# Cross-attention with 16 heads: masks written into the score banks by ScalarE, and held with all 64 keys on 64 rows

## What is computed

```python
# x (4, 1024, 256), ctx (4, 64, 256), mask (4, 1024, 64) of 0 and 1; 16 heads of 16
Q = split_heads(x @ w_q.T + b_q);  K = split_heads(ctx @ w_k.T + b_k);  V = split_heads(ctx @ w_v.T + b_v)
scores = einsum('bhqd,bhkd->bhqk', Q, K) / sqrt(16)
scores = where(mask[:, None] == 0, -1e9, scores)
ctx2 = einsum('bhqk,bhkd->bhqd', softmax(scores), V)      # heads joined again to 256
out = ctx2 @ w_o.T + b_o + x
out = (out - mean(out)) * rsqrt(var(out) + 1e-5) * gamma + beta
```

## Time and profile before

| | us |
|---|---|
| median of 3 runs | 155.9 (155.34 to 156.6) |
| profiled execution, whole | 155.9 |
| its span | 154.0 |
| busy: PE, DVE, POOL, ACT | 136.3, 125.3, 112.3, 94.1 |
| mean granted TensorE clock | 0.978 of full speed |

### The profile page before, as it was taken

The page is one execution under the profiler, slowest core; times in us unless marked ns, Lnnn a source line. Parts: engine busy times, 40 slices in busy tenths (PEclk is TensorE's granted clock), DMA queues, the critical chain, the costliest instruction groups (busy, mean ns, idle before and its releaser), DMA issues.

```text
span 154.0 us, 2935 instructions
## 1 busy us (share of the span) xinstructions
PE 136.3 (89%) x1008; PEld 85.4 (55%) x1008; DVE 125.3 (81%) x232; ACT 94.1 (61%) x166; POOL 112.3 (73%) x107
## 2 busy tenths in 40 slices
PE   0799897978999999999999999999999999999600
PEld 0677755554566646665656565655565455468400
DVE  0296958578879699978997799969998999999991
ACT  3349988867683757297729854783669555380420
POOL 6003748368996069899989999899909989879680
PEclk9999999999999999999999999999999999999965
DMA  5999735999999846208500760018300360200307
GB/s 138 352 302 271 183 88 175 283 304 284 333 237 304 189 135 222 69 0 200 213 2 0 152 261 0 0 34 237 144 0 2 50 227 0 107 33 0 136 2 272
DMA packets 10079, 22.88 MB, mean 149 GB/s; under 512 B 1616, under 2 KB 1872, under 8 KB 10064
## 3 DMA queue, kind: packets, MB, share of 16 engines
q1 hardware_dynamic: 9344, 21.50, 48.9%
q10 hardware_dynamic: 720, 1.19, 2.1%
HBM read 14.82 MB, written 4.19 MB: 123 GB/s over the span
## 4 chain that ended last, share of the span: by engine, by line
PE 67%; DVE 16%; issue 4%; ACT 4%; POOL 4%; DMA 3%; DVEq 1%; POOLq 0%
PE ps_w L402 12%; PE ps_w L357 12%; PE ps_s L436 10%; PE ps_s L465 9%; PE ps_w L491 8%; DVE nmax L750 7%; PE ps_s L442 4%; DVE stat L803 4%; PE ps_s L449 3%; DMA ctx_t<-ctxT 3%; PE ps_w L308 2%; PE ps_w L414 2%; POOL y L994 2%; POOL y L991 2%; PE ps_s L330 1%
## 5 line engine op out<-in xcount | busy, mean ns | idle before, releaser
L750 DVE TENSOR_REDUCE nmax<-ps_w 128x8 f32<-128x512 f32 x56 | 37.7, 683 | 14.1 <-PE ps_w L402 13.5
L649 ACT ACTIVATE probs<-ps_s 128x512 f32<-128x512 f32 x64 | 32.9, 599 | 13.5 <-PE ps_s L449 13.5
L926 POOL TENSOR_TENSOR xt_l<-xt_sb,xt_h 128x1024 fp32r<-128x1024 f32 x7 | 16.6, 2372 | 22.9 <-ACT xt_h L610 17.9
L402 PEld LDWEIGHTS ps_w<-k_half,q_mask 128*128 128x128 f32 x112 | 16.9, 188 | 25.1 <-DVE nmax L750 19.3
L402 PE MATMUL ps_w<-k_half,q_mask 128*128 128x256 f32 x112 | 27.3, 331 | 3.0 <-DVE nmax L750 2.5
L491 PE MATMUL ps_w<-wo_sb,cn 128*128 128x256 f32 x112 | 29.0, 387 | 0.3 <-issue 0.3
L491 PEld LDWEIGHTS ps_w<-wo_sb,cn 128*128 128x128 f32 x112 | 19.4, 189 | 5.8 <-issue 2.5
L617 ACT ACTIVATE q_sb<-ps_w,con 128x512 f32<-128x512 f32 x13 | 8.9, 686 | 21.7 <-PE ps_w L357 21.7
L962 POOL TENSOR_TENSOR x_sb<-x_sb,brow 128x1024 f32<-128x1024 f32 x8 | 19.0, 2375 | 2.3 <-DMA x_sb<-x 2.1
L770 DVE STREAM_TRANSPOSE turned<-ps_s 128x1024 f32<-128x1024 f32 x16 | 19.8, 1240 | 0.2 <-PE ps_s L465 0.2
L991 POOL TENSOR_TENSOR y<-y,brow 128x512 f32<-128x512 f32 x13 | 16.6, 1279 | 4.1 <-ACT y L662 3.8
(11 more groups left out here) (78 smaller groups left out, 197.3 us busy)
## 6 DMA issues: line engine op xcount, KB each, us to landing
m_sb<-maskT SPq DMA_DIRECT2D x32, 128.0 KB, 6.8
x_sb<-x SPq DMA_DIRECT2D x8, 512.0 KB, 5.1
xt_sb<-xT SPq DMA_DIRECT2D x7, 512.0 KB, 7.0
q_mask<-mask SPq DMA_DIRECT2D x24, 128.0 KB, 4.0
out<-y SPq DMA_DIRECT2D x6, 512.0 KB, 3.6
xt_sb<-xT SPq DMA_DIRECT2D x2, 256.0 KB, 5.1
q_mask<-mask SPq DMA_DIRECT2D x8, 64.0 KB, 2.1
out<-y ACTq DMA_DIRECT2D x2, 256.0 KB, 2.2
```

The source lines that it names most:

```text
L402: mm = pe.matmul(max_bank(c, i)[:, half * 256:half * 256 + 256], q_mask[:, c % 2, half, j, t * P:(t + 1) * P], k_half[:, b % 2, half, j].r ...
L649: act.activation(probs[:, g % 2, quad], ps_s[:, quad], ACT.Exp).then_inc(e_done, 1)
L750: dve.tensor_reduce(nmax[:, c % 2, t].rearrange("p (q r) -> p q r", r=32)[:, :, 2 * j:2 * j + 2], max_bank(c, i).rearrange("p (q h k) -> p ...
```

## The change

ScalarE writes the mask of group g+1 into each quad as soon as that quad's exponential of group g is done (`mask_under`, a `Copy` of `mask` from SBUF to the PSUM bank). The bank's keys-by-queries matmul of group g+1 no longer starts an accumulation, it adds to what ScalarE wrote; it waits for its own quad (`under_done`). The eight mask matmuls of a group are gone, but for group 0, which has four from 64 rows. The mask now holds all 64 keys on 64 rows, twice: `mask` and `m_sb` are half as wide, a chunk is loaded by two DMAs, not four, and copied beside the queries by two. `m_first` is gone, its place in the DMA queue is taken by `load_mask(0)`. From step 2 on, `high_x(s+3)` on ACT moves behind `exponentials(s, 1)` and `queries_beside(s+2, 0)`, and `low_x(s+3)` on POOL behind `deviations(s-2)`.

```diff
-        m_sb = sb("m_sb", [P, NI, 2, CHUNK], I32)
-        mask = sb("mask", [P, NM, 2, CHUNK], F32R)
-        m_first = sb("m_first", [P, CHUNK], I32)
+        m_sb = sb("m_sb", [P, NI, CHUNK], I32)
+        mask = sb("mask", [P, NM, CHUNK], F32R)
...
             def load_mask(c):
-                for quad in range(QUADS):
-                    sp.dma_start(m_sb[quad_rows(quad), c % NI], maskT[c].rearrange("(a k) n -> k a n", a=2)
-                                 ).then_inc(in_mask[c % NI], 16)
+                for half in range(2):
+                    sp.dma_start(m_sb[rows(half), c % NI], maskT[c]).then_inc(in_mask[c % NI], 16)
...
             def copy_mask(c):
-                for quad in range(QUADS):
+                for half in range(2):
+                    r = rows(1 - half)
...
-            for half in range(2):
-                sp.dma_start(m_first[rows(half)], maskT[0]).then_inc(in_mfirst, 16)
+            load_mask(0)
             load_xt(1)
             sp.dma_start(wv_sb[:], wv).then_inc(in_wv, 16)
-            load_mask(0)
...
                     pe.wait_ge(qe_done, g + 1)
-                    pe.wait_ge(e_done, QUADS * g)
+                if g == 0:
+                    pe.wait_ge(mask_done, masks_done(0))
+                    for quad in range(QUADS):
+                        r = rows(quad % 2)
+                        pe.matmul(ps_s[:, quad], key_rows[r].rearrange("p h k -> p (h k)"), mask[r, 0],
+                                  start=True, stop=False)
                 for quad in range(QUADS):
                     r = quad_rows(quad)
+                    if g >= 1:
+                        pe.wait_ge(under_done, QUADS * (g - 1) + quad + 1)
                     pe.matmul(ps_s[:, quad], k_pair[r, b, j].rearrange("p h k -> p (h k)"), q_sb[r, c % NQ, j],
-                              start=True, stop=False)
-                pe.wait_ge(mask_done, masks_done(c))
-                for a in range(2):
-                    for quad in range(QUADS):
-                        r = quad_rows(quad)
-                        pe.matmul(ps_s[:, quad], key_rows[r, a].rearrange("p h k -> p (h k)"), mask[r, c % NM, a],
-                                  start=False, stop=False)
+                              start=False, stop=False, skip_group_check=g > 0)
...
                     act.activation(probs[:, g % 2, quad], ps_s[:, quad], ACT.Exp).then_inc(e_done, 1)
+                    if quad and g < GROUPS - 1:
+                        mask_under(g + 1, quad - 1)
+                if g < GROUPS - 1:
+                    mask_under(g + 1, QUADS - 1)
+
+            def mask_under(g, quad):
+                if quad == 0:
+                    act.wait_ge(mask_done, masks_done(g // 2))
+                act.wait_ge(e_done, QUADS * (g - 1) + quad + 1)
+                act.activation(ps_s[:, quad], mask[:, g // 2 % NM].bitcast(F32), ACT.Copy).then_inc(under_done, 1)
...
-                if s + 3 < CHUNKS:
+                if s < 2:
                     high_x(s + 3)
                 if 1 <= s and s + 2 < CHUNKS:
                     queries_out(s + 2, 0)
                 exponentials(s, 1)
                 if s + 2 < CHUNKS:
                     queries_beside(s + 2, 0)
+                if s >= 2 and s + 3 < CHUNKS:
+                    high_x(s + 3)
...
-                if s + 3 < CHUNKS:
+                if s < 2:
                     low_x(s + 3)
                 if s >= 1 and new_batch(s):
                     half_keys(new_batch(s))
                 with_bias(s)
                 if s >= 2:
                     deviations(s - 2)
+                if s >= 2 and s + 3 < CHUNKS:
+                    low_x(s + 3)
                 if s + 3 < CHUNKS:
                     mask_values(s + 3)
```

More of the change, by code:

```diff
@@ L39 @@
 KEY_ROWS = SELECT + 4
-BIAS = KEY_ROWS + 2 * KEYS
+BIAS = KEY_ROWS + KEYS
 CONSTS = BIAS + 4
@@ L63, in build @@
         wq_l = sb("wq_l", [P, PC, D], F32R)
-        key_rows = sb("key_rows", [P, 2, 2, KEYS], F32R)
+        key_rows = sb("key_rows", [P, 2, KEYS], F32R)
         select = sb("select", [P, 2, 2, KEYS], F32R)
@@ L111, in build @@
         in_first = [sem(f"in_first{d}") for d in range(PC)]
-        in_bv, in_mfirst, mfirst_done = sem("in_bv"), sem("in_mfirst"), sem("mfirst_done")
+        in_bv, mfirst_done = sem("in_bv"), sem("mfirst_done")
         in_xt = [sem(f"in_xt{i}") for i in range(2)]
@@ L125, in build @@
         e_done, neg_done, y_done = sem("e_done"), sem("neg_done"), sem("y_done")
+        under_done = sem("under_done")
         wql_done, kt_done, vbd_done, nm_done = (sem(n) for n in ("wql_done", "kt_done", "vbd_done", "nm_done"))
@@ L239, in copy_mask @@
                     sp.wait_ge(max_done, HALVES * (c - 1))
-                for quad in range(QUADS):
-                    r = quad_rows(quad)
-                    sp.dma_start(q_mask[r, c % 2, 1 - quad // 2].bitcast(F32),
-                                 mask[r, c % NM, quad % 2].bitcast(F32).unsqueeze(1).to_broadcast([32, 2, CHUNK])
+                for half in range(2):
+                    r = rows(1 - half)
+                    sp.dma_start(q_mask[r, c % 2, half].bitcast(F32),
+                                 mask[r, c % NM].bitcast(F32).unsqueeze(1).to_broadcast([64, 2, CHUNK])
                                  ).then_inc(mk_in[c % 2], 16)
@@ L247, in copy_first_mask @@
                 sp.wait_ge(mask_done, masks_done(1))
-                for quad in range(QUADS):
-                    r = quad_rows(quad)
-                    sp.dma_start(q_mask[r, 1, 1 - quad // 2, j].bitcast(F32), mask[r, 1, quad % 2].bitcast(F32)
-                                 ).then_inc(landed, 16)
+                for half in range(2):
+                    r = rows(1 - half)
+                    sp.dma_start(q_mask[r, 1, half, j].bitcast(F32), mask[r, 1].bitcast(F32)).then_inc(landed, 16)
             def store(c):
@@ L369, in max_scores @@
                     elif c == 1:
-                        pe.wait_ge(mk_first, 16 * QUADS)
+                        pe.wait_ge(mk_first, 32)
                     else:
-                        pe.wait_ge(mk_in[c % 2], 16 * QUADS * (c // 2 + c % 2))
+                        pe.wait_ge(mk_in[c % 2], 32 * (c // 2 + c % 2))
                     pe.wait_ge(khalf_done, 2 if c == 0 else 4 * (b + 1))
@@ L378, in max_scores @@
                 elif (c, i) == (1, TILES):
-                    pe.wait_ge(mk_in[1], 16 * QUADS)
+                    pe.wait_ge(mk_in[1], 32)
                 if t == 0:
@@ L417, in scores, with scores_on_mask @@
             def scores(c, j):
-                scores_and_mask(c, j)
+                scores_on_mask(c, j)
                 scores_less_max(c, j)
-            def scores_and_mask(c, j):
+            def scores_on_mask(c, j):
                 g = 2 * c + j
@@ L449, in scores_less_max @@
                     pe.matmul(ps_s[:, quad], select[r, j].rearrange("p h k -> p (h k)"), neg[r, c % 2],
-                              start=False, stop=True).then_inc(s_done, 1)
+                              start=False, stop=True, skip_group_check=(c, j) != (0, 0)).then_inc(s_done, 1)
             def values(c, j):
@@ L579, in _ @@
             max_scores(LAST, 7)
-            scores_and_mask(LAST, 0)
+            scores_on_mask(LAST, 0)
             output(LAST - 2, 0, 0)
@@ L677, in _ @@
             queries_out(0, 1)
-            act.activation(key_rows[:], con[:, KEY_ROWS:KEY_ROWS + 2 * KEYS].rearrange("p (a k) -> p a k", a=2)
-                           .unsqueeze(2).to_broadcast([P, 2, 2, KEYS]), ACT.Copy).then_inc(const_done, 1)
+            act.activation(key_rows[:], con[:, KEY_ROWS:KEY_ROWS + KEYS].unsqueeze(1).to_broadcast([P, 2, KEYS]),
+                           ACT.Copy).then_inc(const_done, 1)
             act.activation(select[:].rearrange("p j h k -> p (j h) k"),
@@ L839, in first_mask_values @@
             def first_mask_values():
-                dve.wait_ge(in_mfirst, 32)
+                dve.wait_ge(in_mask[0], 32)
                 for half in range(2):
                     r = rows(1 - half)
-                    dve.tensor_scalar(q_mask[r, 0, half], m_first[r].unsqueeze(1).to_broadcast([64, 2, CHUNK]), 0.0, -BIG,
+                    dve.tensor_scalar(q_mask[r, 0, half], m_sb[r, 0].unsqueeze(1).to_broadcast([64, 2, CHUNK]), 0.0, -BIG,
                                       ALU.is_equal, ALU.mult).then_inc(mfirst_done, 1)
             def mask_values(c):
-                dve.wait_ge(in_mask[c % NI], 16 * QUADS * (c // NI + 1))
+                dve.wait_ge(in_mask[c % NI], 32 * (c // NI + 1))
                 dve.tensor_scalar(mask[:, c % NM], m_sb[:, c % NI], 0.0, -BIG,
@@ L929, in mask_values @@
             def mask_values(c):
-                pool.wait_ge(in_mask[c % NI], 16 * QUADS * (c // NI + 1))
+                pool.wait_ge(in_mask[c % NI], 32 * (c // NI + 1))
                 pool.wait_ge(mask_done, c)
@@ L1066 @@
     consts[row, HALF_BLOCK + row % 64 // DK] = 1
-    for a in range(2):
```

(2 more changed lines are left out.)

## The result

The change makes the kernel slower by half a per cent: 156.58 us (median of 20 runs, 156.12 to 157.34) against 155.82 (20 runs, 155.14 to 156.84), ratio 1.0052, 95% interval 1.0033 to 1.0071. The forecast was 155.9, no change. The profiled execution has a span of 154.9 us, against 154.0.

The account below looks back on a forecast made before the run. The prediction took PE to set the step, with DVE close behind, and ACT to lead at the start. Its terms, +1.1 (start), -2.1 (steps) and +1.0 (tail), summed to 0.0, so 155.9 us, range 153.9 to 158.4.

Parts of the forecast that it names:

- The price of a copy: ScalarE's copy of one mask quad, 128x512 from SBUF to PSUM: forecast 0.53 us from start to start.
- the two rivals that hung on that price: Copies at 0.48 us (154.7 us, chance 0.18), or at 0.60 to 0.64 with ACT the bound (158.3 to 160.3, chance 0.24).
- The cheap copy: Rival: copies cost 0.48 us, giving 154.7 us, or 153.9 if late fourth quads cost nothing at the end; chance 0.18.
- VectorE close behind TensorE: In the repeating steps DVE can take only 0.3 and 0.15 us, so a step falls from 16.1 to about 15.65.
- TensorE's 7 us: PE time of fifteen groups' mask matmuls; the rival with PE as bound counted it in full, 148.9 us, chance 0.10.
- The start: Steps 0 and 1, where ACT leads: copies delay `neg` of chunk 1, the first output and step 2 by 1.1 us.
- The tail: From step 6 to the end: copies between exponentials lose 0.55 us again, and the 0.45 won in step 6.
- a late fourth quad: In the last groups, the next exponential can follow 0.95 us after the last mask is in.
- high_x: On ACT, its old place would have delayed `queries_out(s+2, 0)`, for which an output on PE waits.
- The sum: Whole kernel: +1.1 at the start, -2.1 in the steps, +1.0 at the end, together 0.0 us.

## Why the prediction was wrong, point by point

**The price of a copy**, 0.53 us: right (0.52 to 0.53), and with it the two rivals that hung on that price are out. The cheap copy did not come, ACT did not become the bound of a step.

**VectorE close behind TensorE**: right as a mechanism, and the run without a mask shows it: TensorE's 7 us were never to be had. The size was off, 15.77 for 15.65 a step. What failed here is that the prediction counted only two waits for PE on DVE's row and let the row run on undisturbed. It missed the wait the other way, `output(s-1, 0, 0)` for `cn`, which before lay just behind PE's own work. The timeline of PE and then DVE after:

```profile
91.08 1.13 PE L490 MATMUL ps_w<-wo_sb,cn 128*128 128x256 f32 x4 [0.46 <-DVE cn L794]
```

```profile
91.53 0.73 DVE L814 BATCH_NORM_STATS2 stat<-res 128x6 f32<-128x256 f32 x2
92.29 0.25 DVE L818 BATCH_NORM_AGGREGATE mv<-stat 128x2 f32<-128x6 f32 x2
92.49 0.69 DVE L761 TENSOR_REDUCE nmax<-ps_w 128x8 f32<-128x512 f32 x1
93.35 0.69 DVE L802 TENSOR_TENSOR res<-ps_w,x_sb 128x512 f32<-128x512 f32 x1 [0.17 <-PE ps_w L490]
```

PE is held 0.46, is late with the output, and DVE then waits 0.17 in the middle of the row that in the earlier trace rows had no wait. The four steps win 1.37 us instead of 1.65, 0.3 less than forecast.

**The start**, +1.1: measured +1.27 with the cause named, ScalarE's own chain to `neg` of chunk 1. The first output of the kernel did not wait for `queries_out(3, 0)`, as the prediction had it, but 0.73 us for `cn`, which comes from the same lateness over the maxima and the division.

**The tail**, +0.55: measured +1.56. This is the step of the prediction that failed: 1.0 of the 1.5 us by which the sum was off. The prediction's chain was right link by link until the exponentials of group 13 (5.37 us after those of group 12, forecast 5.34). That the times themselves agree as well (120.79, forecast 120.87) is luck: the start and the steps had lost some 0.45 us more than forecast, and the first exponential had come 0.56 earlier. Behind group 13 its terms were too small. The prediction gave a late fourth quad 0.95 us from its last mask to the next exponential. The timeline of PE after shows the quads of group 15 one by one, with ScalarE's last two copies at 132.06 for 1.14:

```profile
131.88 2.06 PE L441 MATMUL ps_s<-q_sb,k_pair 32*128 32x512 f32 x6
133.26 0.50 PE L448 MATMUL ps_s<-neg,select 4*128 4x512 f32 x2
133.27 0.59 PE L441 MATMUL ps_s<-q_sb,k_pair 32*128 32x512 f32 x1
133.30 0.79 PE L448 MATMUL ps_s<-neg,select 4*128 4x512 f32 x1
133.79 0.59 PE L441 MATMUL ps_s<-q_sb,k_pair 32*128 32x512 f32 x1
133.81 0.79 PE L448 MATMUL ps_s<-neg,select 4*128 4x512 f32 x1
134.53 1.09 PE L464 MATMUL ps_s<-probs,v_bd 64*32 64x512 f32 x16
```

The last mask is in at 133.20, the next exponential starts at 134.48: 1.28. A plain float32 quad is two records, and alone they start 0.52 apart (133.27, 133.79); together, four quads share 1.07. From the last mask of group 14 (in at 125.04) to its exponentials it took 4.05 us, through outputs and `turn_max(7)`, where 3.7 was forecast, and they start at 129.09, not 128.7. Another 0.12 lies between the exponentials of group 13 and the last mask of group 14 (4.25, forecast 4.13). The division, DVE's, confirms the sum: it waits for PE, where the earlier trace rows had no wait, and VectorE stays 0.70 late up to its last instructions, which start at 149.94 instead of 149.24.

```profile
135.91 1.25 DVE L781 STREAM_TRANSPOSE turned<-ps_s 128x1024 f32<-128x1024 f32 x1 [0.84 <-PE ps_s L464]
```

The last 0.2 us of the tail has nothing to do with the copies. In all eleven profiles of kernels with the mask on 64 rows the span ends 0.27 to 0.30 us behind VectorE's closing instruction, and in the three with the old mask 0.03; a closing instruction of SyncE comes that much later. The versions without late copies have it too, so their tails, 40.81 and 40.88, are that of the kernel before, 40.62, and this 0.2. Why it comes later is not known.

**high_x**: wrong in its reason. Its old place would not have held up the output (that one waits for `cn` until later), it holds up GpSimd. The prediction had counted GpSimd's part as covered, in the order after the change, and did not ask what the old order would have done to it.

**The sum** came out as zero from three terms of one to two us each, whose errors all had the same sign: 0.2 in the start, 0.3 in the steps, 1.0 in the tail. The range, 153.9 to 158.4, holds 156.58, but the forecast of no change was wrong: the kernel is slower by half a per cent, and the interval is clear of one.

## What to carry to other kernels

Here work that was moved from a full engine to one with idle time cost nothing where the step repeats, but 0.9 us at the start, where the receiving engine leads, and 1.3 in the tail, where the next piece waits for its last copy: look at the first and the last rounds by themselves, and leave the work there where it was. (The runs gave those rounds four matmuls from 64 rows; the old eight from 32 rows were not run together with the copies. By the start of the version with copies for 4 to 12, 26.09 for 25.72, up to 0.4 us would be left to win there, an estimate.) As it is, 36 of the 60 copies win 0.7 per cent, and all 60 lose 0.5. Before crediting work taken off the fullest engine, follow the ring of waits once round in both directions; leaving the work out altogether shows the ceiling in one run.

## What the runs showed of the hardware

Four matmuls from 64 rows cost 0.66 us between matmuls from 128 rows and from 32 (the run without copies), eight from 32 rows 0.47 among others from 32 rows, for the same columns. Four 32-row tiles of plain float32 share 1.07 us for 512 columns; one that becomes ready alone has its two passes 0.52 apart. A copy from SBUF to a PSUM bank between two exponentials costs 0.52, an exponential from PSUM 0.48.

The granted clock of TensorE fell from its upper level (2.4 GHz) to its lower (1.2 GHz) in some executions at the same place, for 3.4 us shortly after the first exponentials. In the last 0.5 to 0.7 us before the fall matmuls had followed each other without a gap. Just ahead of them TensorE had waited 0.55 and 0.29 us for VectorE, but so it had in the profile of the kernel before, whose clock stayed up. The kernel before with the short bn_stats had a mean of 0.65 from 24 to 28 us, and a projection matmul's starts there are 0.43 apart (25.32, 25.75), not 0.23. Its start stretch is 27.26 us against 25.72 at full clock, 1.5 us, which is twice the effect of this change. Two profiles of kernels with all copies had the same fall (the one with short bn_stats 0.61 from 24 to 28 us) and the start stretch of the kernel after, 26.96 against 26.99: where ScalarE leads, a slow TensorE cost nothing. The times of executions without a profile fit this. Those of the kernel before with a mean clock of 0.970 or less, 8 of 65, took 156.5 to 157.0 us against medians of 155.5 to 155.9; with copies for 4 to 12 it was 4 of 12, at 155.3 to 155.6 against a median of 154.4; with all copies and the moments moved 3 of 10, at 156.0 to 156.4 against 156.45. What makes the clock fall in some executions and not in others stays open.
